# Two one-hot tables built by scalar comparisons, one choice at a time, in a gated attention and mixture-of-experts kernel

## The reference, cut to what matters

```
x = x + tanh(g_xattn[0]) * sliding_window_attention(layernorm(x), ctx, ctx)
x = x + tanh(g_ffn[0])   * moe(layernorm(x), 32 experts, 8 per token, one shared expert)
x = x + tanh(g_xattn[1]) * bidirectional_attention(layernorm(x), ctx)
x = x + tanh(g_ffn[1])   * moe(layernorm(x), 8 experts, 2 per token, shared experts)
```

## Time and profile before

| | |
|---|---|
| median of three runs | 1096.98 us |
| the profiled execution's own time | 1101.13 us |
| span in its profile | 1099.3 us |
| busy: PE, PEld | 930.9 us (85%), 713.5 us |
| busy: DVE, ACT, POOL | 694.2 us (63%), 440.9 us, 539.9 us |
| mean granted clock of PE | 0.921 of 2.4 GHz |

### The profile page before, as it was taken

The page is one execution under the profiler, slowest core; times in us unless marked ns, Lnnn a source line. Parts: engine busy times, 40 slices in busy tenths (PEclk is TensorE's granted clock), DMA queues, the critical chain, the costliest instruction groups (busy, mean ns, idle before and its releaser), DMA issues.

```text
span 1099.3 us, 20610 instructions
## 1 busy us (share of the span) xinstructions
PE 930.9 (85%) x5516; PEld 713.5 (65%) x5517; DVE 694.2 (63%) x2004; ACT 440.9 (40%) x1030; POOL 539.9 (49%) x575
## 2 busy tenths in 40 slices
PE   3458888887699999999999917979999998999893
PEld 2357777776545888888888504645656564787672
DVE  5669999997674865555555247765868246443334
ACT  4548888893052444444444302122222313232220
POOL 7246665644004755555653577875700000786651
PEclk9679999998757999999999967979999998999997
DMA  8960000003101776777768737342300011466647
GB/s 243 216 128 2 1 0 0 0 1 105 46 1 47 224 221 202 224 217 218 211 198 139 282 97 275 102 140 88 112 11 20 1 52 29 87 111 116 143 83 244
DMA packets 75225, 127.44 MB, mean 116 GB/s; under 512 B 12480, under 2 KB 52032, under 8 KB 75008
## 3 DMA queue, kind: packets, MB, share of 16 engines
q0 software_dynamic: 21264, 48.02, 19.2%
q1 hardware_dynamic: 32240, 57.47, 17.2%
q10 hardware_dynamic: 21632, 20.85, 5.4%
HBM read 80.62 MB, written 36.77 MB: 107 GB/s over the span
## 4 chain that ended last, share of the span: by engine, by line
PE 58%; DVE 19%; DMA 7%; issue 7%; POOL 5%; ACT 2%; SPq 2%; DVEq 0%; ACTq 0%; POOLq 0%
PE bank L914 17%; PE bank L929 9%; PE bank L1600 5%; DVE ptl L618 4%; PE bank L903 4%; DMA sw<-in_w 3%; PE bank L810 3%; POOL yg L1193 3%; PE bank L1500 3%; PE bank L424 2%; DVE nmax L610 2%; PE bank L922 2%; PE bank L1535 2%; PE bank L1657 2%; PE bank L1560 2%
## 5 line engine op out<-in xcount | busy, mean ns | idle before, releaser
L1178 POOL DMA_INDIRECT xg<-token_rows,gather_idx x198 | 190.1, 960 | 314.2 <-DMA token_rows<-cw 134.3
L914 PE MATMUL bank<-sw,xgt 128*128 x948 | 244.9, 381 | 0.5 <-issue 0.5
L914 PEld LDWEIGHTS bank<-sw,xgt 128*128 128x128 f32 x948 | 165.4, 191 | 15.5 <-issue 0.8
L1193 POOL DMA_INDIRECT yg<-slot_rows,slot_of x128 | 139.0, 1086 | 67.3 <-issue 34.1
L1007 ACT ACTIVATE ssil<-bank 128x128 f32<-128x128 f32 x237 | 65.7, 278 | 199.9 <-PE bank L914 199.9
L929 PE MATMUL bank<-sw,sht 128*128 x474 | 144.8, 388 | 0.0
L1099 DVE COPY xgt<-bank 128x256 f32<-128x256 f32 x198 | 83.8, 424 | 85.0 <-PE bank L903 75.2
L1112 DVE COPY sht<-bank 128x128 f32<-128x128 f32 x237 | 69.0, 291 | 105.9 <-PE bank L922 105.5
L546 ACT ACTIVATE prob<-bank,nmax 128x256 f32<-128x256 f32 x256 | 111.7, 511 | 8.0 <-DVE nmax L610 8.0
L424 PE MATMUL bank<-consts,prob 128*128 128x128 f32 x512 | 82.6, 285 | 37.3 <-DVE ptl L618 35.0
L610 DVE TENSOR_REDUCE nmax<-bank 128x2 f32<-128x512 f32 x128 | 87.6, 685 | 17.7 <-PE bank L411 17.2
(11 more groups left out here) (218 smaller groups left out, 1648.6 us busy)
## 6 DMA issues: line engine op xcount, KB each, us to landing
slot_rows<-ysb ACTq DMA_DIRECT2D x79, 256.0 KB, 3.3
sw<-in_w SPq DMA_DIRECT2D x48, 384.0 KB, 3.6
kst<-khl SPq DMA_DIRECT2D x32, 224.0 KB, 6.0
token_sums<-zeros SPq DMA_DIRECT2D x2, 2176.0 KB, 12.2
token_rows<-xn SPq DMA_DIRECT2D x8, 512.0 KB, 3.9
sums<-token_sums SPq DMA_DIRECT2D x8, 512.0 KB, 7.2
xg<-token_rows,gather_idx POOLq DMA_INDIRECT x198, 3.5
x<-in_x SPq DMA_DIRECT2D x4, 512.0 KB, 6.8
```

Source lines behind the costliest of these rows:

```text
L914: mm = pe.matmul(bank[2 + k % 2][:, 0:2 * FF], xgt[:, i % 3, c * P:(c + 1) * P], w[:, :, c, :], start=(c == 0), stop=(c == CH - 1))
L1178: nc.gpsimd.indirect_dma_start(xg[:, (first + i) % XG_RING, 0:ROW[L]], None, rows[L], bass.IndirectOffsetOnAxis(gather_idx[:, i:i + 1], 0) ...
L1193: nc.gpsimd.indirect_dma_start(yg[:, t % Y_TILES, j, :], None, ybuf[L], bass.IndirectOffsetOnAxis(slot_of[:, t, j:j + 1], 0)).then_inc(s_y ...
```

## The change

Both tables are laid out with the choice outside: `hot_tok` is `[P, HOTS, 8, P]` and `hot_hi` `[P, HOTS, 8, 160]`, so one choice's elements lie side by side. For each tile and choice DVE now runs two instructions with one tensor input: a comparison of `iota_lo` (128 elements) with the pointer scalar `posl`, multiplied in the same instruction by the pointer scalar `token_id`, which writes `hot_tok`; and a comparison of `iota_col` (159 or 39 elements) with the pointer scalar `posh`. The step on ACT goes, and PE waits for DVE. `iota_lo` and `iota_col` hold one value per slot and per block instead of 8 copies, `iota_lo` in a tile of its own. `posl` and `posh` become 32-bit. After the sigmoid of the router ACT computes the silu of one column into a tile that nobody reads.

```
-        iota_lo = band_f32[:, 2 * DIM:4 * DIM].bitcast(F16).rearrange("p (a j) -> p a j", j=8)
-        iota_col = sb("iota_col", [P, BLOCKS[0], 8], F16)
+        iota_lo = sb("iota_lo", [P, P], F16)
+        iota_col = sb("iota_col", [P, BLOCKS[0]], F16)
+        unread = sb("unread", [P, 1], F32)
...
-        posl = sb("posl", [P, TILES, 8], F16, rt)
-        posh = sb("posh", [P, TILES, 8], F16, rt)
-        hot_lo = sb("hot_lo", [P, HOTS, P, 8], F16, rt)
-        hot_tok = sb("hot_tok", [P, HOTS, P, 8], F16, rt)
-        hot_hi = sb("hot_hi", [P, HOTS, BLOCKS[0], 8], F16, rt)
+        posl = sb("posl", [P, TILES, 8], F32, rt)
+        posh = sb("posh", [P, TILES, 8], F32, rt)
+        hot_tok = sb("hot_tok", [P, HOTS, 8, P], F16, rt)
+        hot_hi = sb("hot_hi", [P, HOTS, 8, BLOCKS[0] + 1], F16, rt)
...
-                pe.wait_ge(m.hots, m.n["hots"] + t + 1)
+                pe.wait_ge(m.hot, m.n["hot"] + t + 1)
                 for j in range(top):
-                    mm = pe.matmul(bank[5][:, P:P + cols], hot_tok[:, t % HOTS, :, j], hot_hi[:, t % HOTS, 0:cols, j],
+                    mm = pe.matmul(bank[5][:, P:P + cols], hot_tok[:, t % HOTS, j, :], hot_hi[:, t % HOTS, j, 0:cols],
...
-        def hots_by_token(act, L, m, tiles):
-            top = (TOP0, TOP1)[L]
-            for t in tiles:
-                act.wait_ge(m.hot, m.n["hot"] + t + 1)
-                if t >= HOTS:
-                    act.wait_ge(m.hotf, m.n["hotf"] + t - HOTS + 1)
-                nc.scalar.activation(hot_tok[:, t % HOTS, :, 0:top], hot_lo[:, t % HOTS, :, 0:top], ACT.Copy,
-                                     scale=token_id[:, t:t + 1]).then_inc(m.hots, 1)
...
             nc.scalar.activation(sc[:, :, :], lg[:, :, :], ACT.Sigmoid).then_inc(m.ra, 1)
-            hots_by_token(act, 0, m, range(TILES))
+            act.wait_ge(m.lgl, 1)
+            nc.scalar.activation(unread[:, :], tg[:, 0:1], ACT.Silu)
...
-                nc.gpsimd.iota(iota_lo[:, :, :], [[1, P], [0, 8]], base=0, channel_multiplier=0,
+                nc.gpsimd.iota(iota_lo[:, :], [[1, P]], base=0, channel_multiplier=0,
                                allow_small_or_imprecise_dtypes=True)
-                nc.gpsimd.iota(iota_col[:, :, :], [[1, BLOCKS[0]], [0, 8]], base=0, channel_multiplier=0,
+                nc.gpsimd.iota(iota_col[:, :], [[1, BLOCKS[0]]], base=0, channel_multiplier=0,
...
-                nc.vector.tensor_tensor(hot_lo[:, t % HOTS, :, 0:top], iota_lo[:, :, 0:top],
-                                        posl[:, t:t + 1, 0:top].broadcast_to([P, P, top]), ALU.is_equal)
-                op = nc.vector.tensor_tensor(hot_hi[:, t % HOTS, 0:cols, 0:top], iota_col[:, 0:cols, 0:top],
-                                             posh[:, t:t + 1, 0:top].broadcast_to([P, cols, top]), ALU.is_equal)
+                for j in range(top):
+                    nc.vector.tensor_scalar(hot_tok[:, t % HOTS, j, :], iota_lo[:, :], posl[:, t, j:j + 1],
+                                            token_id[:, t:t + 1], ALU.is_equal, ALU.mult)
+                    op = nc.vector.tensor_scalar(hot_hi[:, t % HOTS, j, 0:cols], iota_col[:, 0:cols],
+                                                 posh[:, t, j:j + 1], None, ALU.is_equal)
                 op.then_inc(m.hot, 1)
```

More of the change, by code:

```diff
@@ L281, in gated_xattn_moe_kernel @@
             "hot": 16,
-            "hots": 16,
             "hotf": 15,
@@ L316, in __init__ @@
                 self.hot = own["hot"]
-                self.hots = own["hots"]
                 self.hotf = own["hotf"]
@@ L1146, in tables @@
                 pool.wait_ge(s_tabs, 1)
-                nc.gpsimd.tensor_scalar(before[:, :], iota_lo[:, :, 0], part_id[:, 0:1], None,
+                nc.gpsimd.tensor_scalar(before[:, :], iota_lo[:, :], part_id[:, 0:1], None,
                                         ALU.is_gt).then_inc(s_tabs, 1)
@@ L1339, in gather_lists @@
             link(nc.vector.tensor_reduce(incl[0:ne, :], diag[0:ne, 0:ne], AX_X, ALU.add))
-            nc.vector.tensor_scalar(started[0:ne, 0:cols], iota_col[0:ne, 0:cols, 0], incl[0:ne, 0:1], None,
+            nc.vector.tensor_scalar(started[0:ne, 0:cols], iota_col[0:ne, 0:cols], incl[0:ne, 0:1], None,
                                     ALU.is_ge).then_inc(m.bexp, 1)
@@ L1724, in scalar_a1 @@
                 shared_silu(b, u)
-            hots_by_token(act, 1, m, range(TILES))
         def vector_a1(dve, root, m, first, routing, tables):
```

## The result

The changed kernel takes 1112.62 us (median of four runs, 1106.95 to 1117.88) beside 1096.84 (1095.36 to 1097.93): ratio 1.0135, interval 1.0091 to 1.0178. It is slower, and 7.2 us above the forecast of 1105.4. The profiled execution shown here took 1117.15 us; its span is 1115.3 us, 16.0 more than before. In e2 one of ten executions took 1392.8 us at a granted clock of 0.641, in a slow state; it counts in e2's median of 1095.43 us (1094.78 without it) and in no ratio.

A forecast was written before the change was run, and what follows sets the result against it. The prediction took PE's 128 table matmuls (36.91 us) as the bound and DVE as the next; 12.5 + 3.7 - 6.9 - 0.9 = +8.4 us on the median 1097.0 gave 1105.4 us, range 1099 to 1117.

The forecast's parts named there:

- The tables of L = 0: First one-hot to last matmul: DVE becomes the bound, 52.1 us against 39.57, +12.5 us.
- The tail of the last tile: Last tile's eight matmuls behind the last one-hot: between 0 and 2.3 us, taken as 1.2.
- the price per pair: DVE's two one-hot instructions per choice in the L = 0 table: 0.215 and 0.183 us, together 0.40.
- the halving for 16-bit elements: DVE's one-input 16-bit instructions: 0.27 ns per element, half the 32-bit pace of 0.55.
- The tables of L = 1: Twelve tiles on DVE take 8.8 us instead of 5.1: +3.7 us.
- The front: Normalisations to router logits: shorter iotas end PE's idle 3.1 us and a kept clock adds 3.8, -6.9 us.
- The collision: POOL's long iotas slow DVE's four normalisations; short ones bring these from 5.02 to 1.9 us, 3.1 less.
- I take it that it keeps it: 3.8 more, -6.9 in all: Transposes and logits in the front: PE without gaps keeps 2.4 GHz, 4.8 us instead of 8.65.
- the rival of the fallen clock: PE's clock falls during the front all the same, 3.8 us of the gain go, 1109.2 us; chance 0.15.
- The load: Silu table load on ACT moves beside the routing; of its 1.28 us, -0.9 us counts (0 to -1.28).
- free pointers: Rival on DVE's 256 table instructions: pointer scalars cost nothing, a pair 0.22 us, 1078 us; chance 0.10.
- 32-bit pace: Rival on DVE's tables: one-input 16-bit instructions run no faster than 32-bit, +10.2 and +1.1, 1116.7 us; chance 0.15.

The follow-up runs named there:

- e2: Kernel before, with POOL's constant tables (the iotas) moved behind the last normalisation: 1095.43 us, ratio 0.9968.
- e5: Changed kernel plus three unused matmuls behind each of the first fifteen tiles of the L = 0 table: 1109.82 us, ratio 1.0143.
- e4: Changed kernel plus six groups of eight DVE instructions at its end; pitches with no, one, two pointer scalars 0.102, 0.163, 0.223 us for 128 elements.
- e6: Kernel before with iotas moved, early silu load, and hot_hi choices 0 to 3 interleaved by fours, 4 to 7 side by side: 1080.91 us, ratio 0.9876.
- e3: Changed kernel with eleven instead of five unused matmuls behind the attention: 1108.71 us, ratio 1.0106.
- e10: Kernel before with hot_hi interleaved by fours, iotas behind the last normalisation and iota_col four wide: 1075.44 us, ratio 0.9790.
- e7: Kernel before with only the silu of one column added behind the sigmoid: 1098.20 us, ratio 1.0010.
- e1: Changed kernel run again without any edit: 1110.85 us, ratio 1.0122.
- e11: Changed kernel with two long interleaved iotas, into tiles nobody reads, ahead of its short ones: 1115.31 us, ratio 1.0146.

## Why the prediction was right in its sign and short in size

**The tables of L = 0: right.** +12.5 forecast, +12.27 and +12.28 measured; a pair 0.40 us, DVE without gaps, PE waiting, 51.9 us instead of 52.1. The tail of the last tile was 1.25 us (1.2); that was luck, as the 1.2 was the middle of 0 to 2.3 and the tail hangs on the clock: 0.73 us at 2.4 GHz in e5. The place where the new bound would arise, the price per pair and the halving for 16-bit elements all held, and e4 gives the price by itself. The 0.26 us read for a matmul at 2.4 GHz is wrong (0.29, see e6), which the sum does not use.

**The tables of L = 1: right.** +3.7 forecast, +3.55 measured.

**The front: the mechanism right, the clock wrong.** The collision went as forecast (the normalisations 1.59 us, 1.9 forecast). The step that failed is "I take it that it keeps it: 3.8 more, -6.9 in all". PE did run without a gap and was yet at 1.2 GHz in the execution shown, and there nothing of the front's gain was left: not -3.1, as the rival of the fallen clock had it, but 0, since the two batches ahead of the last were slowed as well (1.76 and 3.25 us in the chain instead of 1.07 and 1.87). Over the eight traces whose iotas were out of the way the front took 17.4 to 17.5 us in five, 19.8 and 19.9 in two and 24.8 in one; with the iotas of before it took 24.8 in all four. So the trace's gain is 5.8 us in the mean. What parts them stands in the rows of the granted clock: in the five it fell while PE waited ahead of the first transposes, 0.2 to 0.6 us before their start, was back by the first logits and held to the last; in the other three it fell only after their start, 1.7 us after it in the execution shown, 9.1 in e3, 9.3 in e4, and stayed low to the end of the logits and beyond. What decides in one execution when it falls was not found: the wait was 2.90 us in both executions of the changed kernel, and e3, which filled it, only put the fall off. In the time the gain is 1.2 to 2.6 us in the changed kernel, with intervals that overlap, 3.5 in e2 and 6.2 in e10. Why the time has less than the traces stays open. The traces do not show it lost before the tables of L = 1: from the attention's end to the first one-hot there, less the front and the stage of the first table, 597.5 us pass in the mean of the five traces with the short front and 597.7 in the five with 24.8 us. But each kernel has one or two traces, and executions differ by some us in the attention and in the last stretches.

**The load: the fifth gather mis-sized.** -0.9 forecast; the first silu did come earlier (-1.25), but in e7 0.04 us of it is left at the eleventh. I had let the load count where the fifth block starts, with a gather of 2.69 us; that row is the third gather's, and in e7 the fifth took 3.35, so that its transposes come 0.28 us sooner and not 0.94. What takes the rest of it back by the fifth silu is not shown. Some tenths may remain: in the traces where the clock did not fall behind the first gather, the way from there to the eleventh silu takes 23.2 to 23.8 us in five with the early load and 25.0 in a sixth (e6), 23.9 to 24.2 in the five without it.

**The start of the sparse blocks: not in the sum.** +2 to +3 us in two of the traces (the one shown and e4's, against e1's), at most 1.3 in the others.

**The sum.** With what was measured: 12.3 + 3.6 = 15.8, confirmed by e11's +16.0, less a front of 1.2 to 2.6 in the time. The forecast had 16.2 less 7.8. All of the miss is in the terms subtracted. The rivals on the price of DVE (free pointers, 32-bit pace) are excluded by e4; the 1116.7 of the latter lies near some runs, but for another reason. The range had its upper end from that rival, so it is partly luck that the time, with the front's gain mostly lost, lies inside it.

## What to carry to other kernels

Before an operand is laid out for its reader, price the writer: here PE's matmul went from 0.29 to 0.13 us or less and stood idle, because 32 instructions became 256 with 0.07 us fixed and 0.06 per pointer scalar each. Look for the layout between the two that the writer gets for nothing: choices by fours instead of eights cost DVE no time and gave the stage 15.5 us. A gain that hangs on PE's granted clock is a gain of some executions; put it into the range and not into the sum, above all if it is the term that softens a loss.

## What the runs showed of the hardware that was not expected

- A pointer scalar costs DVE 0.06 us per instruction, for 128 elements as for 512.
- A matmul of 159 columns with a 16-bit moving operand takes 0.29 us from start to start with elements 16 bytes apart and 0.15 us with 8, at either granted clock; only side by side does it follow the clock (0.13 us at 1.2 GHz, 0.07 at 2.4).
- An iota of 1024 16-bit elements takes 1.94 us if each value stands eight times in a row, and 1.03 if the run of values is written eight times.
- PE was busy without a gap for 18 us (258.83 to 277.18 in the execution shown) and stayed at 1.2 GHz from 259.2 on, though a second execution of the same program had 2.4 GHz from 261.4 to the end of the logits.
